# Routed slots and the end of a fused two-layer kernel: bias rows in three buffers, the second w2 half rounded behind the first pair, the last scan step in halves

## The reference

```python
xn = layernorm(x)
# scan part: 4 mixtures m of width 256
g, v, d = xn @ Wg[m] + bg[m], xn @ Wv[m] + bv[m], xn @ Wd[m] + bd[m]
h = linear_scan(sigmoid(g) * tanh(v), a=0.001 + 0.998 * sigmoid(d))      # along the 4096 rows
att = sum(comb[:, m] * h[m])                                             # comb: top 2 of 4, softmax
# routed part: each row goes to one of 8 experts
top = argmax(xn @ gate_w.T + gate_b + expert_bias)
ffn = relu(xn @ w1[top] + b1[top]) @ w2[top] + b2[top]                   # 256 -> 1024 -> 256
out = x + att + ffn
```

## Time and profile before

| | |
|---|---|
| median of 3 runs | 1055.35 us (1053.69 to 1055.56) |
| the profiled execution | 1056.41 us, its span 1054.6 us |
| PE busy | 1029.5 us (98%), weight loads 920.0 us (87%) |
| DVE busy | 753.7 us (71%) |
| ACT busy | 626.4 us (59%) |
| POOL busy | 366.9 us (35%) |
| mean granted clock of PE | 0.996 of full speed |

### The profile page before, as it was taken

The page is one execution under the profiler, slowest core; times in us unless marked ns, Lnnn a source line. Parts: engine busy times, 40 slices in busy tenths (PEclk is TensorE's granted clock), DMA queues, the critical chain, the costliest instruction groups (busy, mean ns, idle before and its releaser), DMA issues. The chain is left out here.

```text
span 1054.6 us, 19932 instructions
## 1 busy us (share of the span) xinstructions
PE 1029.5 (98%) x6564; PEld 920.0 (87%) x6564; DVE 753.7 (71%) x1264; ACT 626.4 (59%) x1138; POOL 366.9 (35%) x305
## 2 busy tenths in 40 slices
PE   6999999999999999999999999999999999999996
PEld 5898898989889898898877888899999999888885
DVE  4875756656575576767769879877777677488788
ACT  4553544444444454545565656788888888566664
POOL 2444453444444344343453783000000000264441
PEclk9999999999999999999999999999999999999998
DMA  5207111010111201513156266578877876332314
GB/s 162 91 17 239 41 40 60 0 64 35 40 60 40 85 15 40 181 61 140 41 202 259 93 214 243 199 241 264 273 264 249 276 249 210 126 125 100 116 58 139
DMA packets 74847, 141.07 MB, mean 134 GB/s; under 512 B 9904, under 2 KB 42544, under 8 KB 73776
## 3 DMA queue, kind: packets, MB, share of 16 engines
q1 hardware_dynamic: 65872, 126.94, 35.1%
q0 software_dynamic: 3072, 8.39, 2.4%
q10 hardware_dynamic: 5856, 5.15, 1.5%
HBM read 101.86 MB, written 38.60 MB: 133 GB/s over the span
## 5 line engine op out<-in xcount | busy, mean ns | idle before, releaser
L734 POOL TENSOR_TENSOR acc<-acc,ytmp 128x512 f32<-128x512 f32 x120 | 156.4, 1303 | 245.9 <-ACT ytmp L823 227.3
L1439 ACT ACTIVATE act_o<-ps,scan_bias 128x512 f32<-128x512 f32 x192 | 130.1, 688 | 106.5 <-PE ps L380 90.9
L823 ACT ACTIVATE ytmp<-ps,sel 128x256 f32<-128x256 f32 x256 | 107.6, 472 | 100.4 <-PE ps L1041 99.8
L889 DVE SCALAR_TENSOR_TENSOR hT_l<-ps,hT_h 128x512 fp32r<-128x512 f32 x128 | 87.7, 685 | 104.1 <-ACT hT_h L786 103.9
L1039 PE MATMUL ps<-vals_h,hT_h 128*128 128x256 f32 x512 | 145.2, 284 | 0.8 <-DVE hT_l L889 0.7
L1040 PE MATMUL ps<-vals_l,hT_h 128*128 128x256 f32 x512 | 143.6, 280 | 0.0
L1041 PE MATMUL ps<-vals_h,hT_l 128*128 128x256 f32 x512 | 143.5, 280 | 0.0
L786 ACT ACTIVATE hT_h<-ps 128x512 fp32r<-128x512 f32 x128 | 76.5, 598 | 96.1 <-PE ps L380 95.9
L1580 POOL DMA_INDIRECT y_b<-y_d,pos_i x20 | 25.6, 1280 | 290.0 <-DMA y_d<-y_sb 267.1
L925 DVE SCALAR_TENSOR_TENSOR acc<-ps,sel,acc 128x256 f32<-128x256 f32 x240 | 104.0, 474 | 3.0 <-PE ps L1041 2.9
L1703 DVE TENSOR_TENSOR_SCAN h_b<-a_b,hstate,xs_b 128x512 f32<-128x512 f32 x64 | 90.0, 1406 | 22.2 <-ACT a_b L1444 16.9
(11 more groups left out here) (224 smaller groups left out, 2766.4 us busy)
## 6 DMA issues: line engine op xcount, KB each, us to landing
raw<-w SPq DMA_DIRECT2D x78, 512.0 KB, 5.1
x1T<-xT_d SPq DMA_DIRECT2D x16, 512.0 KB, 4.9
comb_b<-comb_d SPq DMA_DIRECT2D x8, 1024.0 KB, 8.5
w_small<-w SPq DMA_DIRECT2D x14, 512.0 KB, 4.5
xs_d<-zeros ACTq DMA_DIRECT2D x1, 4992.0 KB, 19.6
x_in<-x SPq DMA_DIRECT2D x8, 512.0 KB, 4.0
x_d<-x SPq DMA_DIRECT2D x8, 512.0 KB, 4.5
xn_d<-xn SPq DMA_DIRECT2D x8, 512.0 KB, 2.6
```

What stands on the lines that cost most here:

```text
L734: pool.tensor_tensor(dst[:, 2:4, :], acc[:, 2:4, :], ytmp[:, k % 2, :, :], ALU.add).then_inc(acc23, 1)
L823: act.activation(ytmp[:, k % 2, j - 2, :], yb(k, j), ACT.Copy, scale=sel[:, j, k:k + 1]).then_inc(y_23, 1)
L1439: act.activation(act_o[:, i % 2, w, :], ps[:, 3 * (i % 2) + w, :], func, bias=scan_bias[:, w, i:i + 1]).then_inc(act_g, 1)
```

## The change

- **b1.** `b1c` has three buffers. The row of slot n + 2 is loaded in slot n, and waits for the relus of slot n - 1.
- **w2.** `w2_half(n, 1)` moves from ahead of the first pair to behind it, on ACT and on DVE.
- **Scatters.** On POOL the `mix` of a step comes ahead of that step's scatters.
- **Gathers and late sums.** Every y and every late x has its own buffer (`late_y`, `late_x`, over memory that the slots used). POOL issues all 32 gathers in one go behind the slots, and nothing after. SP loads all late x behind the slots and no longer waits for the stores. `mix` of groups 4 to 6 moves from POOL to DVE. The additions of y to x, and to the first results, are put at eight places in groups 4 to 6 (`LATE_ADDS`), and none is left in group 7.
- **End in halves.** Group 7 is written out on PE and ACT. Its steps no longer copy the last column to `hstate`. Its last step is done in halves of 256 columns on PE (36 matmuls of 256 columns for 18 of 512; the second half in the banks of step 6), ACT and DVE; the transposes and the sums follow in halves, and the second half of the result is stored from ACT's queue.

```diff
-    b1c = rc("b1c", [P, FJ], F32)
+    b1c = rc("b1c", [P, ROUND, FJ], F32)
...
+    late_y = rl("late_y", [P, GROUPS - B_FIRST + 1, JT, D], F32)
+    late_x = rl("late_x", [P, GROUPS - B_FIRST, JT, D], F32)
+    HALF = GT // 2
...
     def mixed_on_dve(g):
-        return isinstance(g, int) and (2 <= g < B_FIRST or g == GROUPS - 1)
+        return isinstance(g, int) and g >= 2
...
 sync:
-            def load_b1(n, e):
+            def load_b1(n, k, e):
+                if not (isinstance(n, int) and n < ROUND):
+                    wait_alone(sp, t_ok, FJ * (n - ROUND + 1))
                 if not zero(n):
-                    wait_alone(sp, t_ok, FJ * n)
-                sp.dma_start(b1c[:], ...)
+                    wait_alone(sp, b1_in, 16 * n)
+                sp.dma_start(b1c[:, k % ROUND, :], ...)
...
-                if left(r, k) > 0:
-                    load_b1(n + 1, expert_at(r, k + 1))
+                if left(r, k) > 1:
+                    load_b1(n + 2, k + 2, expert_at(r, k + 2))
...
+            for g in range(B_FIRST, GROUPS):
+                sp.dma_start(late_x[:, g - B_FIRST], x1_d[g]).then_inc(late_x_in[g - B_FIRST], 16)
...
 tensor:
+            def last_products():
+                g, i = GROUPS - 1, MC - 1
+                for half in (0, 1):
+                    pe.wait_ge(act_g, 3 * (MC * g + i - 1 + half))
+                    t = slice(half * HALF, (half + 1) * HALF)
+                    for w in range(3):
+                        for k in range(DC):
+                            last_mm = mm3(pe, ps[:, 3 * (1 - half) + w, t], ...)
+                        last_mm.then_inc(b_full, 1)
+            def last_rows():
...
+                pe.wait_ge(acc_ok, 6 * g + 5)
+                for j in range(JT):
+                    pe.transpose(side4[:, j, 0:P], accT[:, 0, j * P:(j + 1) * P], ident[:])
+                for half in (0, 1):
+                    pe.wait_ge(acc_ok, 6 * g + 6 + half)
+                    for j in (2 * half, 2 * half + 1):
+                        last_mm = pe.transpose(side4[:, j, P:2 * P], accT[:, 1, j * P:(j + 1) * P], ident[:])
+                    last_mm.then_inc(fin_full, 1)
...
 scalar (step: the last step in halves, with a_b behind the three functions of each half):
             def slot(r, k):
                 n, (_, st) = ROUND * r + k, blocks(r, k)
-                w2_half(n, 1)
                 for q in range(FJ // 2):
-                    relu(n, q, st * P)
+                    relu(n, k, q, st * P)
                     round_e(n, q, st * P)
+                    if q == 0:
+                        w2_half(n, 1)
...
+            act.wait_ge(fin_ok, GROUPS + 1)
+            act.dma_start(out_v[GROUPS - 1][:, 2:4, :], late_sum(GROUPS - 1)[:, 2:4, :]).then_inc(out_st, 16)
 gpsimd:
+                    if i >= DC and not mixed_on_dve(g):
+                        mix(g, i)
                     if isinstance(g, int) and (g, i) in SCATTER_AT:
                         scatter(SCATTER_AT.index((g, i)))
-                    if g >= B_FIRST and i == 4: ...
-                    if B_FIRST <= g < GROUPS - 1 and i == 5: ...
-                    if i >= DC and not mixed_on_dve(g):
-                        mix(g, i)
...
+            for g in (3, 4, 0, 5, 6, 1, 2, 7):
+                index = pos_i[:, g * JT:(g + 1) * JT]
+                gather(first_y or late_y of g, index, ...)
 vector:
+            def last_half(half):
+                # xs_b, scan (carry from hstate or from column 255), hw_b and accT on 256 columns
...
+            LATE_ADDS = {(4, 3): [3], (4, 6): [4], (5, 4): [0], (5, 5): [5], (5, 7): [6], (6, 4): [1], (6, 5): [2],
+                         (6, 7): [7]}
...
             def total(g):
-                dve.tensor_tensor(x1_b[:], x1_b[:], y_b[:], ALU.add).then_inc(fin_sum, 1)
                 dve.wait_ge(fin_sum, g - B_FIRST + 2)
...
             def slot(r, k):
-                w2_half(n, 1)
                 for q in range(FJ // 2):
                     low_e(n, q, st * P)
+                    if q == 0:
+                        w2_half(n, 1)
```

More of the change, by code:

```diff
@@ L1173, in body @@
                     wait_alone(sp, fin_ok, g)
[L1174 to L1178, removed]
+                    if g >= B_FIRST:
+                        sp.dma_start(out_v[g - 1], late_sum(g - 1)).then_inc(out_st, 16)
+                if g < B_FIRST:
+                    sp.dma_start(x1_b[:], x1_d[g]).then_inc(x1b_in, 16)
             def load_late(i):
@@ L1309, in _ @@
             sp.wait_ge(comb_st, 32)
-            with sp.Fori(B_FIRST, GROUPS - 1) as g:
-                body(g)
-            body(GROUPS - 1, True)
+            for g in range(B_FIRST, GROUPS):
+                sp.dma_start(late_x[:, g - B_FIRST], x1_d[g]).then_inc(late_x_in[g - B_FIRST], 16)
+            for g in range(B_FIRST, GROUPS):
+                body(g, g == GROUPS - 1)
             for g in range(B_FIRST - 1):
@@ L1315, in _ @@
                 sp.dma_start(out_v[g], first_res[g]).then_inc(first_st, 16)
[L1316 to L1319, removed]
+            sp.wait_ge(fin_ok, GROUPS)
+            sp.dma_start(out_v[GROUPS - 1][:, 0:2, :], late_sum(GROUPS - 1)[:, 0:2, :]).then_inc(out_st, 16)
             sp.wait_ge(first_st, 16 * (B_FIRST - 1))
@@ L1436, in step @@
                     act.wait_ge(a_ok, n - 1)
+                if last_step(g, i):
+                    for half in (0, 1):
+                        t = slice(half * HALF, (half + 1) * HALF)
+                        for w, func in enumerate((ACT.Sigmoid, ACT.Tanh, ACT.Sigmoid)):
+                            act.wait_ge(b_full, 3 * (n + half) + w + 1)
+                            act.activation(act_o[:, i % 2, w, t], ps[:, 3 * (1 - half) + w, t], func,
+                                           bias=scan_bias[:, w, i:i + 1]).then_inc(act_g, 1)
+                        act.wait_ge(scan_ok, n - 1)
+                        act.wait_ge(act_g, 3 * (n + half) + 3)
+                        act.activation(a_b[:, i % 2, t], act_o[:, i % 2, 2, t], ACT.Copy, scale=0.998,
+                                       bias=0.001).then_inc(a_ok, 1)
+                    return
                 for w, func in enumerate((ACT.Sigmoid, ACT.Tanh, ACT.Sigmoid)):
@@ L1526, in _ @@
             every_slot(slot, act)
-            with act.Fori(B_FIRST, GROUPS) as g:
+            with act.Fori(B_FIRST, GROUPS - 1) as g:
                 for i in range(MC):
                     step(g, i)
+            for i in range(MC):
+                step(GROUPS - 1, i)
+            act.wait_ge(fin_ok, GROUPS + 1)
+            act.dma_start(out_v[GROUPS - 1][:, 2:4, :], late_sum(GROUPS - 1)[:, 2:4, :]).then_inc(out_st, 16)
         @block.gpsimd
@@ L1694, in step @@
                 m, c = divmod(i, DC)
+                if last_step(g, i):
+                    for half in (0, 1):
+                        last_half(half)
+                    return
                 if not zero(g):
@@ L1838, in _ @@
                     step(g, i)
+                    for f in LATE_ADDS.get((g, i), []):
+                        add_y(f)
                     if i == rows_step(g) + 1:
                         total(g - 1)
-                    if g > B_FIRST and i == rows_step(g) + 2:
-                        f = g - B_FIRST - 1
-                        dve.wait_ge(first_y_in[f], 64)
-                        dve.tensor_tensor(first_res[f], first_res[f], first_y[:, f], ALU.add).then_inc(first_ok, 1)
             total(g)
```

104 lines of the change are left out of this document (76 added, 28 removed).

## The result

The changed kernel took 1058.1 us (median of 13 runs, 1056.27 to 1059.7), the kernel before beside it 1055.35 (13 runs, 1053.69 to 1058.79). The ratio is 1.0019 with a 95% interval of 1.001 to 1.0027: slower by a fifth of a per cent, which is clear of 1 by the interval, and above the range given (1050.1 to 1056.7). Run again (e5) it took 1056.95 us, ratio 1.0015 [1.0006, 1.0024]. The profiled execution took 1058.36 us at a span of 1056.6.

A forecast was written before the change was run, and what follows sets the result against it. The prediction took the kernel as bound by PE's issue. From the profiled 1056.41 us, slots +0.2 and end -2.0 gave 1054.6; less that execution's 1.06 over the median, 1053.5 against 1055.35, range 1050.1 to 1056.7.

The forecast's parts named there:

- Late groups and scatters: Groups 4 to 7 with additions moved to DVE, and POOL's reordered scatters: both hidden, worth nothing.
- scan of step 6: Group 7's end: DVE starts this scan on time behind its `a_b`, at 1041.45 instead of 1042.84.
- Rival C: Later load of w2's second half decides, 0.8 us in each of six big slots: 1057.8 us, slower; chance 0.15.
- the forecast's +0.2: All slots together, in us: -2.0 + 3.2 + 0.3 - 1.6 + 0.3.
- 1.6 us of gain: Big slots behind small ones: 2.1 us of PE waits fall to some 0.5, as relu needn't wait for w2's half.
- I cost it at nothing by itself: Bias loaded two slots ahead: takes waits of ACT away, few reaching PE, so no gain of its own.
- costed at 0.05 each: Big slots before small ones: delayed pairs 2 and 3 cost +0.05 us each, +0.3 for all.
- +3.2, +0.3 and +0.3: Costs in us: six small slots +3.2, round 0's small slot +0.3, big slots before small ones +0.3.
- Small slots, 0.54 each: Each small slot becomes 0.54 us longer, since the delayed pairs exceed 0.36 us of slack; six cost +3.2.
- Slot 0, -2.0: Layer 2 of slot 0 starts earlier, at 672.2, at full clock, and ends at 678.5 instead of 680.5.
- The end, -2.0: Group 7's last step: scan on time and work in halves, last sum at 1049.85 instead of 1051.84.
- B: Rival: small slots don't pay for the new order, -3.2 us more, 1050.3 us; chance 0.22.

The follow-up runs named there:

- e5: The changed kernel itself measured again, nothing changed: 1056.95 us, ratio 1.0015.
- e11: The changed kernel with each scatter ahead of POOL's add of its step, as before: 1057.63 us, ratio 1.0021.
- e3: The changed kernel with the second w2 half behind the first pair in small slots alone, ahead elsewhere: 1069.19 us, ratio 1.0081.
- e10: e6 with the bias loaded one slot ahead, behind all relus of the slot, memory for three buffers kept: 1054.75 us, ratio 1.0.
- e6: The changed kernel with the second w2 half ahead of the first pair in every slot and POOL's gathers spaced out: 1052.69 us, ratio 0.9978.
- e4: The kernel before with only the second w2 half put behind the first pair in every slot, one bias buffer: 1079.89 us, ratio 1.0227.
- e13: The changed kernel with POOL's gathers spaced out, the second w2 half still behind the first pair: 1057.7 us, ratio 1.0024.
- e14: The kernel before with only the three bias buffers, loaded two slots ahead: 1054.58 us, ratio 0.9991.
- e17: e6 with the bias buffers moved behind everything else and 32 unused bytes in their place: 1050.92 us, ratio 0.9955.
- e18: The changed kernel with the bias buffers moved as in e17, nothing else: 1057.55 us, ratio 1.0043.
- e8: The changed kernel with the last step of group 7 whole, not in halves: 1057.7 us, ratio 1.0027.
- e12: e6 with 64 unused bytes behind b1c and the second w2 half behind the first pair in slot 0 alone: 1052.6 us, ratio 0.9977.
- e1: The changed kernel with the second w2 half ahead of the first pair in every slot, gathers in one go: 1056.84 us, ratio 0.9993.
- e2: The changed kernel with the second w2 half behind the first pair only in the first slot of each round: 1059.89 us, ratio 1.0045.
- e15: e3 with POOL's gathers spaced out: 1057.4 us, ratio 1.0026.

## Why the forecast missed

**What held.** The kernel is bound by PE, and each moved instruction did what the working said. In small slots the low rows end 7.22 us into the slot, the number worked out. Slot 0 resumes at 672.18 (forecast 672.2) at full clock; it gave 2.4 us for 2.0, though not all by the order (below). Late groups and scatters cost nothing in the changed kernel (e11, and 34.5 us per group), though the gathers in one go, also put at nothing, go with losses of up to 13.3 us in its variants (e3). The scan of step 6 is on time. Rival C (the later load in all big slots) did not happen: they behave alike from slot 9 on.

**Where it failed: the slots, +2.95 us for the forecast's +0.2, and the end, -1.4 for -2.0.** The failed step is the price of the two parts of the change in the slots: the order was given 1.6 us of gain that the runs do not show it to have, and too small a cost, and the bias buffers were put at nothing. By its own terms:

- **b1, "I cost it at nothing by itself".** It is worth 2.3 us with the half ahead (e10 against e6) and is what keeps the new order from costing 20 (e4). The waits in big slots behind small ones, 1.6 us of gain, went into the sum as the work of the order. With the buffers there, the order takes nothing off these six slots: 71.75 us in e13, 71.60 in e6. e14 takes 2.2 us off them with the half left ahead. So the order was credited with a gain that comes without it. That it is all the buffers' is not shown: e10 has 71.6 us there too, with the late load. The working also had 2.1 us to win in these slots; by the starts it was 3.1 (73.47 less six times 11.72, the least of them).
- **Their size, no term at all.** 64 bytes more moved the halves of the weights and made the products slower, some 0.1 us in each big slot. e17 gains 2.4 us on e6 by the ratios, 1.25 by the slots; e18's slots are 2.3 us shorter than the changed kernel's, 1.2 shorter than those of e5. It explains most of the usual excess of the big slots in front of small ones, costed at 0.05 each and 0.12: with the half ahead they take 11.61 (e6).
- **The order.** Its terms were -2.0, +3.2, +0.3 and +0.3, and the -1.6 of above, in all +0.2; alone it costs 4.9 (e13 against e6). By the starts these are 3.5 in six small slots, 0.5 in that of round 0, 1.3 in slots 4 and 13, 0.15 in the six big ones behind small ones, and -0.55 in slot 0.
- **Small slots, 0.54 each.** Measured 0.66. The missing 0.12 lies between `sT_l` and PE's next product. I had 0.13 us there; it is 0.25 in the five small slots behind which the rolled loop jumps back (7.47), and 0.12 to 0.13 less in the one behind which it is left (7.34). That the jump takes it, now that PE has no work queued ahead, fits both but was not tried.
- **Single big slots, no term.** Slot 1 took 0.95 us more here, 0.3 in e5, and nothing against the half ahead in e8 and e13 (11.66); but in e13 slot 4 took 12.50. A half of w1 is late in them (ACT waits 0.79 us for it in slot 1 here, 0.76 in slot 4 of e13), whose load follows the pairs of the slot before. e12 shows it with the order changed in slot 0 alone (slot 1 11.61 to 12.15, slot 2 7.52 to 8.41). I had looked for what is late next in small slots only.
- **Slot 0, -2.0.** The size was right in this pair of traces, but 1.5 of it was the clock, which e6 keeps with the half ahead and e1 does not, and 0.4 came without the order (15.99 us in the kernel before, 15.59 in e1). What the order itself gives there is 0.5 us.
- **The end, -2.0.** The scans of 256 columns took 0.75 us for the 0.70 taken, and the last addition started 0.48 us after its product; why is open. The halves alone give 0.6 to 0.75 us (e8).

In steps, by the ratios: the buffers with what they push are 0.9 us faster (e14 against the kernel before), the rest of the change with the half ahead and spaced gathers 1.4 faster (e6 against e14), the order 4.9 slower (e13 against e6). That is 2.5 us slower; the changed kernel itself is 1.6 to 2.8 us slower than the one before. Each step is uncertain by about 1 us.

In the list of rivals, B's time is 1050.3 by its own sum, not the range's 1050.1; nothing hangs on it.

The forecast also took the excess of the profiled execution of before over its median, 1.06 us, as common to both kernels. If it lay in the waits that the change removes (slot 12 alone took 13.16 us in it, its neighbours of the kind 11.7 to 12.3), 1 us of gain was counted that a median run does not have. That is argued, not shown.

**What stays open:** why the address matters; why some executions lose 1.4 to 13.3 us in groups 4 and 5 (traces of e2, e1 and e3) when all gathers go in one go, and others none; and by what way POOL's gathers hold ACT up. Above 1060 us lie 3 of 12 runs of e1, 6 of e2, 8 of e3, 5 of e18 and 1 of the 11 of e8, none of the 24 of the changed kernel; with spaced gathers, 1 of e13 and 2 of e15, of which no trace tells. Of the 65 runs of spaced kernels with the half ahead, or behind in first slots alone, none lies above 1057 us.

## What to carry to other kernels

When one edit brings a new buffer and a new order, price each alone with the other left as it was: here the gain came without the order, and the order had the cost. In this kernel rounding a loaded weight belongs in the time in which the engine would wait for the first product; behind it, it delays a chain that a small slot has no room for. When a buffer grows in the middle of an allocation, look at what it pushes: place new bytes behind the operands that the bound engine reads, and compare the starts of its products, not its waits.

## What the hardware showed that was not expected

- Matmuls on weights 64 bytes further up ran slower with no wait in the trace: slots of 6.81 and 11.50 us became 6.88 and 11.61 (e14), and came back when the weights' place was put back by moving the bias buffers away (e17).
- The same 1.94 us of idle ahead of the same matmul left the granted clock at 1.00 in one execution and at 0.57 over the next 4 us in another (e6, e1). The Trainium skill (TensorE: Matmul & The Clock Gate, section "What's actually happening") calls the count of slow matmuls at a kernel's start run-variable; here it is so in its middle. A gain that rests on the clock is a gain in some executions.
- With 32 indirect gathers in one go on POOL, ACT idled 4.95 us with its product done, and groups 4 and 5, 34.5 us each, took 37.7 and 44.5 (e3); spaced out, they took 34.5 in every trace, in one go too in the changed kernel.
